# Query rows kept and loaded once, doubled on the chip by GpSimd, and a minimum per half of each score sum

## What is computed

```python
x = x + 0.5 * ffn(layernorm(x))          # three 256x256 products in a row, bias, tanh
x = x + attn(layernorm(x))
x = x + 0.5 * ffn(layernorm(x))

# attn:
content = einsum('bihd,bjhd->bhij', q + u_bias, k)
pos = relative_shift(einsum('bihd,jhd->bhij', q + v_bias, p))   # p = positions @ Wp
probs = softmax((content + pos) * dh ** -0.5)
out = einsum('bhij,bjhd->bihd', probs, v) @ Wo + bo
```

## Time and profile before

| | us |
|---|---|
| median of 3 runs | 3401.79 (3401.78 to 3402.23) |
| the profiled execution | 3404.41 |
| its span, first to last instruction | 3402.6 |
| PE busy (matmul) | 3354.7 |
| ACT busy | 2331.2 |
| DVE busy | 1945.1 |
| POOL busy | 1331.3 |

### The profile page before, as it was taken

One profiled execution on the slowest core, in us unless ns is written; L12 is line 12 of the kernel. 1 busy time (PEld: TensorE's weight loads), 2 busy tenths in 40 slices (PEclk: granted clock), 3 DMA queues, 4 the chain that ended last, 5 costly groups with the idle time before them and its releaser, 6 DMA issues. The chain is left out here.

```text
span 3402.6 us, 110393 instructions
## 1 busy us (share of the span) xinstructions
PE 3354.7 (99%) x34876; PEld 2084.5 (61%) x34876; DVE 1945.1 (57%) x5651; ACT 2331.2 (69%) x3255; POOL 1331.3 (39%) x1341
## 2 busy tenths in 40 slices
PE   8998999999999999999999999999999999999998
PEld 5674666666666666666666666666666666666677
DVE  7872555555555555555555555555555555555567
ACT  3343777777777777777777777777777777777643
POOL 2211444444444444444444444444444444444410
PEclk9997999999999999999999999999999999999999
DMA  5989999999999999999999999999999999999862
GB/s 167 283 255 310 400 388 389 390 386 388 390 388 388 389 388 388 388 389 389 388 387 391 387 389 386 390 388 386 391 389 388 387 389 385 391 388 389 332 202 97
DMA packets 433553, 1231.27 MB, mean 362 GB/s; under 512 B 48992, under 2 KB 133472, under 8 KB 433504
## 3 DMA queue, kind: packets, MB, share of 16 engines
q1 hardware_dynamic: 429424, 1228.07, 96.2%
q10 hardware_dynamic: 4080, 2.58, 0.3%
HBM read 617.04 MB, written 613.43 MB: 362 GB/s over the span
## 5 line engine op out<-in xcount | busy, mean ns | idle before, releaser
L902 POOL TENSOR_SCALAR at_pos_in<-at_pos_in,at_neg_max 128x1024 f32<-128x1024 f32 x1024 | 1149.2, 1122 | 1682.4 <-DVE at_neg_max L865 1682.4
L827 ACT ACTIVATE at_pos_out<-at_ps_pos 128x1024 f32<-128x1024 f32 x1019 | 1045.2, 1026 | 504.6 <-PE at_ps_pos L739 504.6
L865 DVE CUSTOM_DVE_ANT_0 at_pos_in<-at_ps_con,at_pos_in 128x512 f32<-128x512 f32 x1024 | 708.7, 692 | 1171.5 <-PE at_ps_con L739 802.1
L739 PE MATMUL at_ps_con<-keep_right,keep_left 32*128 32x512 f32 x4116 | 1337.9, 643 | 2.1 <-ACT at_pos_out L827 1.1
L836 ACT ACTIVATE at_prob<-at_ps_turn 128x512 f32<-128x512 f32 x2048 | 1112.0, 595 | 282.3 <-PE at_ps_turn L772 240.7
L739 PE MATMUL at_ps_pos<-keep_right,keep_left 32*128 32x512 f32 x4076 | 1155.6, 643 | 12.9 <-PEq L97 12.9
L772 PE MATMUL at_ps_turn<-keep_ident,at_pos_in 128*128 128x128 f32 x8192 | 1105.6, 278 | 0.0
L772 PEld LDWEIGHTS at_ps_turn<-keep_ident,at_pos_in 128*128 128x128 f32 x8192 | 891.0, 141 | 155.7 <-issue 153.4
L785 PEld LDWEIGHTS at_ps_pv<-at_prob,keep_v_aug 128*32 128x32 f32 x16384 | 385.0, 109 | 773.6 <-issue 773.5
L865 DVE CUSTOM_DVE_ANT_0 at_pos_in<-at_ps_con,at_pos_in,at_neg_half 128x512 f32<-128x512 f32 x1024 | 769.2, 751 | 134.9 <-PE at_ps_con L739 0.4
L785 PE MATMUL at_ps_pv<-at_prob,keep_v_aug 128*32 128x128 f32 x16384 | 659.3, 279 | 0.8 <-issue 0.8
(11 more groups left out here) (96 smaller groups left out, 1380.4 us busy)
## 6 DMA issues: line engine op xcount, KB each, us to landing
scratch_scores<-at_pos_out SPq DMA_DIRECT2D x1024, 512.0 KB, 8.0
at_pos_in<-scratch_scores SPq DMA_DIRECT2D x1024, 512.0 KB, 8.4
keep_left<-scratch_queries SPq DMA_DIRECT2D x127, 256.0 KB, 8.1
scratch_queries<-fr_qk SPq DMA_DIRECT2D x124, 256.0 KB, 4.0
fr_x<-in_L_attn_x_dram SPq DMA_DIRECT2D x16, 512.0 KB, 7.4
scratch_x<-fr_x_bo SPq DMA_DIRECT2D x16, 512.0 KB, 4.9
scratch_keys<-fr_qk SPq DMA_DIRECT2D x32, 256.0 KB, 5.5
scratch_values<-fr_values SPq DMA_DIRECT2D x8, 1024.0 KB, 5.8
```

The lines of the kernel that those rows point to most:

```text
L739: return pe.matmul(banks[:, n, :], left[side][rows, t.i * P:(t.i + 1) * P], right[side][rows, :], start=True, stop=True)
L827: act.activation(pos_out[:, t.slot, :], banks[:, :, :].rearrange("p a m -> p (a m)"), ACT.Copy)\
L865: dve.tensor_tensor_reduce(pos_in[:, t.slot, keys], ps_con[:, n, :], pos_in[:, t.slot, keys], -SCALE, 3.0e38 if n == 0 else neg_half[:, t. ...
L902: pool.tensor_scalar(pos_in[:, t.slot, :], pos_in[:, t.slot, :], -1.0, neg_max[:, t.slot:t.slot + 1], ALU.mult, ALU.add).then_inc(shifted, 1)
```

## The change

`queries` keeps two strips instead of four, and each query block is stored once. In the attention phase a unit's content queries are loaded once, into strip 0 of `left`, and its positional queries once, into strip 2, by two DMAs of 16 partitions: the positional ones two units ahead, at step 0, the content ones one unit ahead, at step 2 (the keys stay at step 1, the values move to step 3). GpSimd copies strip 2 to strip 3 after tile 4 and strip 0 to strip 1 after tile 6, and TensorE waits for these copies (`pos_twice`, `con_twice`) in place of the loads. On VectorE, each half of a tile takes its own minimum, the second half no longer waits for the first, and a third instruction, a tensor_tensor of 128x1, takes the minimum of the two; GpSimd waits for that (`lowest`). `scored`, which TensorE waits for, is still given by the two sums.

```diff
--- before.py
+++ after.py
@@ -37,7 +37,7 @@
 HEAD_RING, X1_RING, X2_RING = 3, 4, 5
 X_RING = 5
 BIAS_LOADS, VECTOR_LOADS = 4, 14
-QK_STORES = 5 * C
+QK_STORES = 3 * C
 
 
 def at_once(eng, sem, value):
@@ -165,9 +165,8 @@
         def store_queries(eng, g, o):
             k, slot, half = g % 2, g // 2 * H + 1 - o, DH // C
             for c in range(C):
-                for strip in (2 * o, 2 * o + 1):
-                    eng.dma_start(a["queries"][slot:slot + H, strip, c * half:(c + 1) * half, k * ROWS:(k + 1) * ROWS],
-                                  qk[k][:, o, c, :]).then_inc(qk_out[k], 16)
+                eng.dma_start(a["queries"][slot:slot + H, o, c * half:(c + 1) * half, k * ROWS:(k + 1) * ROWS],
+                              qk[k][:, o, c, :]).then_inc(qk_out[k], 16)
 
         steps = range(-4, GROUPS + 1)
 
@@ -210,10 +209,10 @@
                     for k in range(2):
                         sp.wait_ge(qk_out[k], 16 * QK_STORES)
                     sp.wait_ge(v_out[0], 16)
-                    query_rows = a["queries"].rearrange("n s d m -> n (s d) m")
-                    sp.dma_start(keep["left"][1][2 * STRIP:P:2, :], query_rows[0, STRIP:2 * STRIP, :])\
-                        .then_inc(keep["first_in"], 16)
-                    sp.dma_start(keep["left"][0][0:P:2, :], query_rows[1]).then_inc(keep["q_in"][0], 16)
+                    for n in range(2):
+                        sp.dma_start(keep["left"][1 - n][2 * STRIP:3 * STRIP:2, :], a["queries"][n, 1])\
+                            .then_inc(keep["pq_in"][1 - n], 16)
+                    sp.dma_start(keep["left"][0][0:STRIP:2, :], a["queries"][1, 0]).then_inc(keep["q_in"][0], 16)
                     sp.dma_start(keep["right"][0][0:2 * STRIP:2, :], a["keys"][0].rearrange("n d m -> (n d) m"))\
                         .then_inc(keep["k_in"][0], 16)
                     sp.dma_start(keep["v_in"][0][:, :], a["values"][0, :, :]).then_inc(keep["vals_in"][0], 16)
@@ -556,6 +555,17 @@
                         pool.tensor_copy(keep["right"][1 - k][P // 2:P, :],
                                          keep["pos_keys"][P // 2:P, k * HALF:(k + 1) * HALF]).then_inc(keep["p_ready"], 1)
                     pool.wait_ge(keep["p_ready"], 2)
+                if g == GROUPS - 2:
+                    pool.wait_ge(scale2_ready, GROUPS)
+                    for n in range(2):
+                        pool.wait_ge(keep["pq_in"][1 - n], 16)
+                        pool.tensor_copy(keep["left"][1 - n][3 * STRIP:P, :],
+                                         keep["left"][1 - n][2 * STRIP:3 * STRIP, :]).then_inc(keep["pos_twice"], 1)
+                    pool.wait_ge(keep["q_in"][0], 16)
+                    pool.tensor_copy(keep["left"][0][STRIP:2 * STRIP, :], keep["left"][0][0:STRIP, :])\
+                        .then_inc(keep["con_twice"], 1)
+                    pool.wait_ge(keep["pos_twice"], 2)
+                    pool.wait_ge(keep["con_twice"], 1)
                 if real(g + 4):
                     pool.wait_ge(variance1_ready, g + 5)
                     pool.tensor_tensor(scale1[g % 2][:, :], variance1[g % 2][:, :], keep["minus_half"][:, :], ALU.pow)\
@@ -584,7 +594,7 @@
 
         pos_out = sb("pos_out", [P, RING, S])
         pos_in = sb("pos_in", [P, RING, S])
-        neg_max, neg_half = sb("neg_max", [P, RING]), sb("neg_half", [P, RING])
+        neg_max, neg_half = sb("neg_max", [P, RING]), sb("neg_half", [P, RING, 2])
         prob = [sb(f"prob{k}", [P, TILES, QUAD * P]) for k in range(2)]
         left, right, v_in, v_aug = (keep[n] for n in ("left", "right", "v_in", "v_aug"))
         head_T = sb("head_T", [P, P])
@@ -594,11 +604,12 @@
         ps_pv, ps_head = psum("ps_pv", [P, P]), psum("ps_head", [P, QUAD, VW])
 
         written, read = sems("written", RING), sems("read", RING)
-        q_in, k_in, vals_in, first_in, p_ready = (keep[n] for n in ("q_in", "k_in", "vals_in", "first_in", "p_ready"))
+        q_in, pq_in, k_in, vals_in, p_ready, pos_twice, con_twice = (
+            keep[n] for n in ("q_in", "pq_in", "k_in", "vals_in", "p_ready", "pos_twice", "con_twice"))
         head_out = keep["head_out"]
-        (pos_mm, pos_copied, con_mm, scored, shifted, turned, exped, pv_mm, pv_copied, head_mm, inverted,
+        (pos_mm, pos_copied, con_mm, scored, lowest, shifted, turned, exped, pv_mm, pv_copied, head_mm, inverted,
          normed, v_ready) = (
-            sem(n) for n in ("pos_mm", "pos_copied", "con_mm", "scored", "shifted", "turned", "exped",
+            sem(n) for n in ("pos_mm", "pos_copied", "con_mm", "scored", "lowest", "shifted", "turned", "exped",
                              "pv_mm", "pv_copied", "head_mm", "inverted", "normed", "v_ready"))
 
         class Tile:
@@ -653,14 +664,15 @@
 
         @block.sync
         def _(sp):
-            def load_queries(u):
+            def load_pos_queries(w):
+                at_once(sp, pos_mm, w.units(TILES, -TILES))
+                sp.dma_start(left[1 - w.side][2 * STRIP:3 * STRIP:2, :], a["queries"][w.unit(), 1])\
+                    .then_inc(pq_in[1 - w.side], 16)
+
+            def load_con_queries(u):
                 if u.past(BODY):
                     at_once(sp, con_mm, u.units(2 * TILES, -2 * TILES))
-                at_once(sp, pos_mm, u.units(TILES))
-                rows = 2 * STRIP if u.last_unit() else P
-                sp.dma_start(left[u.side][0:rows:2, :],
-                             a["queries"][u.unit() + 1].rearrange("s d m -> (s d) m")[0:rows // 2, :])\
-                    .then_inc(q_in[u.side], 16)
+                sp.dma_start(left[u.side][0:STRIP:2, :], a["queries"][u.unit() + 1, 0]).then_inc(q_in[u.side], 16)
 
             def load_keys(u):
                 if u.past(BODY):
@@ -713,7 +725,9 @@
                 back = Tile(r, t + LEAD - READ_LAG)
                 if back.real():
                     read_back(back)
-                for at, load in ((0, load_queries), (1, load_keys), (2, load_values)):
+                if t % TILES == 0 and Tile(r, t + 2 * TILES).real():
+                    load_pos_queries(Tile(r, t + 2 * TILES))
+                for at, load in ((1, load_keys), (2, load_con_queries), (3, load_values)):
                     if t % TILES == at and Tile(r, t - at + TILES).real():
                         load(Tile(r, t - at + TILES))
                 if isinstance(r, int) and r * BODY + t == NT:
@@ -741,7 +755,7 @@
 
             def content(t, n):
                 if n == 0 and t.i == 0:
-                    pe.wait_ge(q_in[t.side], t.r * 16 + 16)
+                    pe.wait_ge(con_twice, t.units(1, 1))
                     pe.wait_ge(k_in[t.side], t.r * 16 + 16)
                 if t.past(1):
                     pe.wait_ge(scored, t.count(2, n - 1))
@@ -754,11 +768,7 @@
             def positional_room(t, buffers=1):
                 if t.i == 0:
                     pe.wait_ge(p_ready, t.units(1, 1))
-                    if t.past(TILES):
-                        u = Tile(t.r, t.t - TILES)
-                        pe.wait_ge(q_in[u.side], u.r * 16 + 16 * (u.unit_in_body // 2 + 1))
-                    else:
-                        pe.wait_ge(first_in, 16)
+                    pe.wait_ge(pos_twice, t.units(1, 1))
                 if t.past(buffers):
                     pe.wait_ge(pos_copied, t.count(1, 1 - buffers))
 
@@ -858,13 +868,12 @@
                         dve.wait_ge(read[t.slot], t.rounds(RING, 1))
                         if t.past(RING):
                             dve.wait_ge(shifted, t.count(1, 1 - RING))
-                    else:
-                        dve.wait_ge(scored, t.count(2, 1))
                     dve.nop(nofuse=True)
-                    low = neg_half if n == 0 else neg_max
                     dve.tensor_tensor_reduce(pos_in[:, t.slot, keys], ps_con[:, n, :], pos_in[:, t.slot, keys], -SCALE,
-                                             3.0e38 if n == 0 else neg_half[:, t.slot:t.slot + 1], ALU.add, ALU.min,
-                                             low[:, t.slot:t.slot + 1]).then_inc(scored, 1)
+                                             3.0e38, ALU.add, ALU.min, neg_half[:, t.slot, n:n + 1]).then_inc(scored, 1)
+                at_once(dve, scored, t.count(2, 2))
+                dve.tensor_tensor(neg_max[:, t.slot:t.slot + 1], neg_half[:, t.slot, 0:1], neg_half[:, t.slot, 1:2],
+                                  ALU.min).then_inc(lowest, 1)
 
             def copy_products(t):
                 dve.wait_ge(pv_mm, t.quads(1))
@@ -898,7 +907,7 @@
         @block.gpsimd
         def _(pool):
             def less_maximum(t):
-                at_once(pool, scored, t.count(2, 2))
+                at_once(pool, lowest, t.count(1, 1))
                 pool.tensor_scalar(pos_in[:, t.slot, :], pos_in[:, t.slot, :], -1.0, neg_max[:, t.slot:t.slot + 1],
                                    ALU.mult, ALU.add).then_inc(shifted, 1)
 
@@ -920,9 +929,28 @@
```

(25 more changed lines are left out.)

## The result

The changed kernel takes 3416.3 us (median of 6 runs, 3413.9 to 3423.7), the kernel before 3402.7 (6 runs, 3401.8 to 3404.1): a ratio of 1.0039, with an interval of 1.0026 to 1.0052. The change makes the kernel 0.4% slower. The prediction was 3323, range 3280 to 3375: wrong in size and in sign.

The account below looks back on a forecast made before the run. It took a loop of PE and VectorE as the bound, DMA engines close behind. 3404.4 - 74 (attention, 22.2 us a unit instead of 22.78) - 5 (first phase) = 3325, as median 3323 us; range 3280 to 3375.

Parts of the forecast that it names:

- The sums: VectorE, attention phase: without the wait between the two halves' sums, `scored` comes 0.24 us earlier, bounds 0.06 and 0.28.
- Rival C: The gap between VectorE's two sums stays without its wait: a unit of 22.54 us, 3367 us in all; chance 0.12.
- The third instruction: VectorE's 128x1 minimum takes 0.15 us and GpSimd starts 3.17 us into the step instead of 3.12; cost zero.
- The copies: GpSimd's two copies per unit take 1.03 us each and make PE late by 0.2 us a unit: 21.9 becomes 22.1.
- rival D: GpSimd's copies set the loop, slower from 1.76 us a copy on; with 1.91, 3418 us in all; chance 0.07.
- The query rows once, and what the transfers allow: Attention-phase loads: 0.13 MB or 1.5% less per unit; transfers allow 22.2 us a unit, saving 74 us over 127 units.
- the term of 22.2: Attention unit as the transfers allow it, 22.78 x (1 - 0.01 - 0.015) us, taken as later than the engines' 22.1.
- 1% to spare: Attention-phase transfers could run about 1% faster, read from a landing time that falls by 0.9 us in 90 us.
- Rival B: The transfers have nothing to spare: a unit of 22.45 us at 388 GB/s, 3355 us in all; chance 0.14.
- The first phase: Fewer query stores at its end save 5 us; the clock of 0.50 between 293 and 330 us stays.

Follow-up runs that it names:

- short reads: The changed kernel with score reads of all tiles but the first 8 cut to 896 of 1024 columns, engines' work unchanged: 3304.0 us, 0.9556 of the kernel before.
- the queries' half alone: The changed kernel with VectorE's part undone, leaving queries once and GpSimd's two copies: 3403.3 us (0.9840), on another chip 3399.5 us (0.9830) of the kernel before.
- the queries in fours: The changed kernel with the query rows loaded as four DMAs of 4 rows each, keys as they were: 3404.6 us, 0.9842 of the kernel before.

## Why the prediction was wrong

1. *The sums.* Right. The gap of 0.22 is gone, the sum takes 688 ns, and `scored` comes 0.30 earlier in the timeline, 0.28 as the median of all steps with short reads, against 0.24 forecast and 0.28 as the bound. Rival C falls: the same instruction starts 0.00 after the start of the accumulator read without the wait and 0.21 after it with the wait. The Trainium skill (VectorE: DVE Perf Modes, "The DRAIN you can't avoid") has the semaphore cost nothing extra, by a measurement of eight tensor_copies; the same section adds that an instruction that isn't held starts earlier, and the prediction left that out. The traces here don't agree with the first and bear out the second: the measurement decides.
2. *The third instruction.* Right in its length, 0.16 us, and in GpSimd's start, 3.10 against 3.17. That it costs nothing is not shown by itself; with short reads the whole loop keeps the forecast pace with it.
3. *The copies.* Right: 1034 and 1029 ns in the changed kernel, 1.03 forecast, far from the 1.76 of rival D. In the loop they cost 0.29 a unit and not 0.2, and the loop without them runs at 21.75 and not 21.9; the two cancel, by luck, so that with short reads the unit is 22.06 against 22.1.
4. *The query rows once, and what the transfers allow.* This is the step that failed. It is the term of 22.2, what the transfers allow, with their 1% to spare: the changed kernel's unit is (3219.7 - 325.6) / 126 = 22.97, from this row:

```profile
L675 SPq DMA_DIRECT2D keep_left<-scratch_queries x127: 570/913/1277, 325.6 to 3219.7; - x127
```

   The 1% to spare was read from a median landing that fell by 0.9 us in a stretch, and the range for the rest from mean rates: 388 GB/s as the rate of a stage without spare, 404 GB/s from a short stretch. Both took a rate that was reached for one that can be kept. When the transfers do bind, the stage moves 378 GB/s, and 8.71 MB take 23.0; that is later than the 22.78 of the kernel before, which carries 1.5% more. Rival B, "nothing to spare", had the right mechanism and took the full rate of 388 for its price (22.45, 3355). The landings of 10.4 us were the queue of one engine that was late already (10.4, where the other fifteen had delivered by 6.4), not of sixteen with room to spare.
5. *The first phase.* Right: attention starts 4.8 us earlier, at 296.13 instead of 300.95, against 5 forecast. The granted clock behind it, from 293 to 330 us, is 0.56 for 0.50: still near the lower of the two levels, 1.2 GHz.

The sum now: 3404.4 + 127 x (22.97 - 22.78) - 5 = 3423.5, and the profiled execution took 3423.7; the median of the six runs, 3416.3, is 7 us below it.

With this the range was wrong on its slow side: the only slower case was rival D, on GpSimd, and no case said that transfers which bind could also slow down. On two of the other chips the change was run against a kernel before that waits for the transfers already; there the fewer bytes tell and the change is 0.7% faster (0.9928 and 0.9929). The engines' part and the bytes are the same on both; the sign depends on whether the kernel before still had its margin.

What stays open is the mechanism of the lower rate. Two changes come together when VectorE catches up: reads are taken the moment they land, and SyncE's queue waits for landed writes (213.4 us, 6.3 before), so that more of its issues follow arrivals, though most of its waits are still for ScalarE's copies (784.2 us, 1005.6 before). That the late engine has moments without work in this state is a guess that fits; no run shows it. Why only one engine of 16 is late, and why the kernel before takes 1.6% longer on the three chips, isn't settled either.

The simplest of the best versions here is the queries' half alone: 0.9840 and 0.9830 of the kernel before on two chips, and 0.9% faster than the whole change in the comparison on one chip (3399.5 against 3431.9). It beats both kernels there; the whole change with the wait back (0.9853) or with the queries in fours (0.9842) is within the intervals of it. On the chip of the result it wasn't run. There the kernel before already ran at its loop's own 22.78 a unit, so little more than the 5 us of the first phase would be left to win, by estimate from that unit.

## What to carry to other kernels

Where a loop of engines sits within a few per cent of the transfers, price the transfers by the slowest DMA engine and by the rate in a stretch where somebody really waits for a landing; a mean share or a rate that was reached for 30 us overstates them. Where the transfers bind, as here, a faster engine is worth nothing and can even cost time; fewer bytes come first. The quickest test of which of the two binds is a kernel that moves a few per cent less and leaves each engine's instructions as they are; its result is then not the program's.
